# Folding weight pairs three steps behind their loads, and a fixed place for VectorE's loop head

## What is computed

```python
h = einsum(silu(gate) * value, w2)          # [3008 tokens, 1024], from g = silu(gate) * value
y = rms_norm(h, post_ln)                    # residual stream, written out
a = layer_norm(y) @ [wq_a | wkv_a].T        # 256 + 64 + 64 columns
q, ckv = rms_norm(a[:, :256]), rms_norm(a[:, 256:320])
k_pe = rope(a[:, 320:384])
```

## Time and profile before

| what | us |
|---|---|
| median of 3 runs (lowest, highest) | 2511.26 (2506.93, 2512.43) |
| the profiled execution, its own time | 2511.18 |
| its span (first to last instruction) | 2509.5 |
| of it: TensorE busy, VectorE busy | 2377.4, 1815.0 |
| this stage: first load of g to the first load of attention | 635.2 to 961.8 |

### The profile page before, as it was taken

One profiled execution on the slowest core, in us unless ns is written; L12 is line 12 of the kernel. 1 busy time (PEld: TensorE's weight loads), 2 busy tenths in 40 slices (PEclk: granted clock), 3 DMA queues, 4 the chain that ended last, 5 costly groups with the idle time before them and its releaser, 6 DMA issues. The chain is left out here.

```text
span 2509.5 us, 45975 instructions
## 1 busy us (share of the span) xinstructions
PE 2377.4 (95%) x14716; PEld 2061.9 (82%) x14716; DVE 1815.0 (72%) x3545; ACT 1246.3 (50%) x3736; POOL 1231.2 (49%) x1017
## 2 busy tenths in 40 slices
PE   8999999988699996999999999999999996999998
PEld 7888878776466676999999999878888885999998
DVE  8875586795446666898889898855776566777775
ACT  5664454442334545999999999922222222111110
POOL 5774675774013225677677767620676553111110
PEclk9999999999899998999999999989999998999999
DMA  7654576667556651111111111287788996211111
GB/s 251 209 175 127 183 258 226 214 227 265 165 170 198 198 188 59 48 43 56 50 55 45 51 56 54 70 284 225 213 252 244 284 288 224 71 68 68 67 67 51
DMA packets 318257, 379.44 MB, mean 151 GB/s; under 512 B 25472, under 2 KB 260480, under 8 KB 317952
## 3 DMA queue, kind: packets, MB, share of 16 engines
q1 hardware_dynamic: 310320, 349.67, 44.3%
q0 software_dynamic: 7184, 25.69, 2.6%
q10 hardware_dynamic: 576, 2.10, 0.3%
HBM read 295.59 MB, written 81.79 MB: 150 GB/s over the span
## 5 line engine op out<-in xcount | busy, mean ns | idle before, releaser
L1551 ACT ACTIVATE attn_prob<-attn_prob,attn_bias 94x94 f32<-94x94 f32 x1024 | 366.8, 361 | 47.3 <-DVE attn_bias L1627 46.0
L668 DVE TENSOR_TENSOR up_t_lo<-early_raw,up_t_hi 128x502 fp32r<-128x502 f32 (+1 forms) x210 | 222.1, 1060 | 142.8 <-ACT up_t_hi L575 140.6
L517 POOL TENSOR_TENSOR early_raw<-early_raw 128x502 f32<-128x502 f32 (+1 forms) x150 | 234.1, 1564 | 133.0 <-DVE up_t_lo L668 73.4
L1672 POOL TENSOR_TENSOR attn_prob<-attn_prob,attn_share 94x752 f32<-94x752 f32 x128 | 188.1, 1470 | 178.6 <-DVE attn_share L1635 178.6
L575 ACT ACTIVATE up_t_hi<-early_raw 128x502 fp32r<-128x502 f32 (+1 forms) x210 | 130.8, 623 | 281.1 <-POOL early_raw L517 158.5
L1911 POOL TENSOR_TENSOR early_raw<-early_raw 128x512 f32<-128x512 f32 x120 | 172.1, 1439 | 194.2 <-DMA early_raw<-o_t 194.0
L1946 DVE TENSOR_TENSOR out_t_lo<-early_raw,out_t_hi 128x512 fp32r<-128x512 f32 x168 | 158.5, 946 | 148.3 <-ACT out_t_hi L1925 147.5
L756 PE MATMUL up_ps<-up_t_lo,early_s_hi 128*128 128x502 f32 (+1 forms) x608 | 243.6, 401 | 18.3 <-DVE up_t_lo L668 16.1
L1925 ACT ACTIVATE out_t_hi<-early_raw 128x512 fp32r<-128x512 f32 x168 | 105.1, 631 | 302.2 <-POOL early_raw L1911 148.1
L757 PE MATMUL up_ps<-up_t_hi,early_s_lo 128*128 128x502 f32 (+1 forms) x608 | 240.5, 396 | 0.0
L758 PE MATMUL up_ps<-up_t_hi,early_s_hi 128*128 128x502 f32 (+1 forms) x608 | 239.8, 394 | 0.0
(11 more groups left out here) (261 smaller groups left out, 6697.0 us busy)
## 6 DMA issues: line engine op xcount, KB each, us to landing
early_raw<-o_t SPq DMA_DIRECT2D x288, 256.0 KB, 4.7
early_raw<-x_f SPq DMA_DIRECT2D x240, 251.0 KB, 3.6
shared_ring<-w SPq DMA_DIRECT2D x120, 256.0 KB, 3.9
early_raw<-x_f SPq DMA_DIRECT2D x120, 250.0 KB, 3.4
shared_ring<-wvo SPq DMA_DIRECT2D x96, 256.0 KB, 4.8
o_t<-attn_o_t SPq DMA_DIRECT2D x128, 188.0 KB, 1.9
shared_ring<-wo SPq DMA_DIRECT2D x32, 512.0 KB, 6.6
y<-early_raw POOLq DMA_DIRECT2D x24, 512.0 KB, 3.6
```

Source lines behind the costliest of these rows:

```text
L517: nc.gpsimd.tensor_tensor(both[n % 2][:, 0:w], a, b, SEVEN[i].op_b).then_inc(both_done, 1)
L668: nc.vector.tensor_tensor(t_lo[s % NT][:, 0:w], src, t_hi[s % NT][:, 0:w], ALU.subtract).then_inc(lo_done, 1)
L1551: last = nc.scalar.activation(prob[u % NPR][0:SEQ, h, part], prob[u % NPR][0:SEQ, h, part], ACT.Exp, bias=bias[u % 2][0:SEQ, n:n + 1], sca ...
L1672: nc.gpsimd.tensor_tensor(p4, p4, share[u % 2][0:SEQ, :].unsqueeze(2).broadcast_to((SEQ, 8, SEQ)), ALU.mult).then_inc(prob_done, 1)
```

## The change

Two values. Folds are done three steps behind their loads in place of two, which moves them to steps 3, 4, 6, 7, ... 21, 22, 24 and 25 on TensorE, ScalarE and GpSimd (SyncE's loads keep their steps). And VectorE's loop in this stage gets a fixed place for its first instruction.

```diff
@@ -877,7 +877,7 @@
         CENTRE_AT = 2
         DEPTH = 4
         U = 6
-        D_F = 2
+        D_F = 3
         FOLD = {0: 0, 1: 1, 3: 2, 4: 3}
         assert PAIRS == TILES // U * len(FOLD)
 
@@ -1198,7 +1198,7 @@
                 body(k, m)
                 link.fill()
 
-            run_steps(dve, TILES, DEPTH, U, step)
+            run_steps(dve, TILES, DEPTH, U, step, at=0)
```

## The result

The changed kernel takes 2613.02 us (median of 4 runs, 2612.14 to 2613.72) against 2510.66 before (4 runs): ratio 1.0408, 95% interval 1.0392 to 1.0425. The profiled execution took 2612.93 us, its span is 101.7 us longer than before. Forecast were 2606 us, 2560 to 2645, and slower with 0.93.

A forecast was written before the change was run, and what follows sets the result against it. TensorE, busy 95% of the span, was taken as the bound. Beginning -6, steps 4 and 5 +13.4, steps 6 to 23 +82.9 (loop head gain included) and end +5 made +95.3, so 2606 us, range 2560 to 2645.

The forecast's parts named there:

- The release a step too late: SyncE's pair load waits for TensorE's fold in the same step, delaying g behind it: three steps 44.7 us, 12.3 more.
- 3k+1: Second step of each group of three, with a fold and late g: 18.7 us before the clock term.
- 3k+2: Third step of each group of three, no fold but late g: 13.0 us.
- The clock: TensorE's lower clock after idle waits: 2.9 us per three steps, 1.8 of it for 3k+1, between 0 and 6.6.
- End: Steps 24 to 27: step 24 lags about 1 us, step 25 carries the last fold, 4 us; together +5.
- Beginning: Step 2 loses its fold and step 3 carries the first: 6 us of gain, between 0 and 8.
- Steps 4 and 5: First steps with late g: 33.5 us in place of 20.1, +13.4.
- Loop head: VectorE's standstills at its loop's back edge, steps 12 and 18, go: full gain of 8.3 us, nothing for the entry.
- A: Rival at the head of 3k+1 and 3k+2: g lands within 5.3 us of release, in time; 2502 us, chance 0.04.
- B: Rival on g's transfer: neighbours could be what costs; landing 6 us after release gives 2508 us; chance 0.03.
- C: Rival: only steps with a fold suffer, 3k+2 staying at 8.0 us; 2559 us, chance 0.08.
- D: Rival: the loop head edit fails and VectorE still stands still twice, 6 us each; 2618 us, chance 0.15.

The follow-up runs named there:

- e10: Changed kernel plus 20 and 14 extra matmuls, results unused, in TensorE's two idle times; 2589.79 us, ratio 1.033 to the kernel before.
- e3: Changed kernel (folds three steps behind, loop head placed) with SyncE issuing g one step earlier; 2498.46 us, ratio 0.9949 to the kernel before.
- e1: Changed kernel with folds back at two steps behind, so only the loop head's place remains; 2501.9 us, ratio 0.9965 to the kernel before.
- e2: Changed kernel without the loop head's fixed place, so only the later folds remain; 2611.21 us, ratio 1.0393 to the kernel before.
- e6: Changed kernel with the two loads of wo left out from the third pair on; 2516.16 us, ratio 1.0024 to the kernel before.
- e8: Changed kernel with folds two steps behind and VectorE's loop head on slot 210 in place of 0; 2506.52 us, ratio 0.9987 to the kernel before.
- e11: e3 without the loop head's fixed place; 2502.05 us, ratio 0.9975 to the kernel before.

## Why the prediction was right

- *The release a step too late.* Right in place, and in size nearly so. In 3k+1 g was to land 12.6 us into the step and fold_v to begin at 14.1; in the step shown they came at 12.9 and 14.1 (813.7 and 814.94, from 800.8), on average of the six at 12.2 and 13.4. TensorE's idle time before it was to be 6.4 and is 5.6 on average (6.5 in the step shown), at the end of 3k+2 4.6 and 4.6. ScalarE waits for g 14 times in steps 4 to 23, 10.2 us each, for 14 times 7 to 10. Without the low clock a group takes 44.55 us for 44.7 forecast (e10). Its terms are less exact: the six 3k+1 of e10 take 19.1, 16.7, 18.6, 16.7, 18.5 and 17.8 us (cut at SyncE's pair loads), 17.9 on average for 18.7 forecast, so that the other two steps have 26.65 for 26.0. The two errors nearly cancel.
- *The clock* was the term that was mis-sized: 2.9 us per group forecast, 3.6 measured. Step 3k+1 takes 20.1 us for 17.9 in e10, so 2.2 for 1.8 forecast, and the other two steps together 28.0 for 26.65, so 1.4 for 1.1. The idle time at the end of 3k+2 is paid for in step 3k: from 784.6 to 800.8 it runs at 0.72 though g is in time there, and it takes 16.2 us. 3k+2 itself (13.05 for 13.0) pays nothing, since it waits for g anyway. Six groups make 4 of the 7 us by which the forecast fell short.
- *End*: +5 forecast, +7.9 measured. I left the clock out of this part: steps 24 and on run at 0.72, before at 0.84. e3, with full steps before it, has +4.3 against before (+4.9 against e1). That the other 3.6 us are the clock's was not tried by itself.
- *Beginning*: -6 forecast, -5.2 measured; e3 shows that -11.7 was to be had where g is not late, beyond the bound of 8 that I gave.
- *Steps 4 and 5*: +11.3 for +13.4. Against this stand +1.5 us ahead of this stage, which the change does not touch and which the forecast put at 0.
- *Loop head*: the gain, 8.1 us for 8.3, is real where VectorE is needed at once (e1: 202.7 to 194.6). As a gain of the changed kernel it is not shown: the forecast of steps 6 to 23 (six groups without a standstill) holds, but e2, with the head as before, is not slower in all, and the 4.7 us more of its trace do not stand in the steps of the back edges. So the groups of 48 us stand with and without the head, and the sum would have been as good had the head done nothing. The two standstills of before are 5.54 and 6.3 us, not 5.5 both. The cost at the entry of the loop, which I put at nothing, is a standstill of 1.9 to 2.7 us (1.9 in the changed kernel, 2.7 in e1); e3 pays 1.4 of its 2.1.
- The sentence that these two are the only standstills at a back edge is too strong: in the last stage VectorE's L2144 has two of up to 2.0 us, shortly behind the back edges of its loop.
- *Rivals.* A (2502 us) is excluded as the case, but its threshold fits with e6, and e1 and e3 are about what it priced. B was wrongly dismissed in its mechanism: with two loads and three quarters of the bytes fewer ahead, g takes 4.5 us in the median in place of 8.2 (the 12 loads of g behind a pair in steps 6 to 23). It did not come true because the loads are there. C is excluded: 3k+2 takes 13.05 us and not 8.0. D priced two standstills at 6 us each on top; in e2, where they could have been, there are two, of 2.6 and 2.5 us, and the total shows nothing of them. The estimate of 2.6 us for g was worked out from a fit that the Trainium skill ("DMA: Bandwidth & Descriptors", "Anatomy of one DMA") gives for a DMA that GpSimd issues, and SyncE issues g. No run here had g alone; the traces have 7.5 to 9.6 us behind six loads and 4.2 to 5.4 behind four. On the head, the Trainium skill ("Runtime: NRT & Kernel Launch", "Instruction fetch mechanics") says that an engine holds two blocks of 256 instructions and fetches first when a branch leads outside them. The runs agree as far as they go: no standstill at the back edge with the loop in two blocks (0 and 70), and up to 6.2 us with three (e8).

## What to carry to other kernels

Before a consumer is moved a step later, follow its release through the in-order queue that it feeds: what costs may be a load that stands behind and has nothing to do with it. Here 2 to 3 in one constant cost about 100 us (e2). The same constant with the small load issued one step ahead gained 6 us (e11), and 12 with the loop head placed too (e3). A loop head is worth placing where the trace shows the engine standing still at the back edge with nothing to wait for (8 us in e1), and where g was late no gain of it is resolved.

## What the runs showed that I had not expected

- The cost of a late load does not grow in proportion: landings 6.4 to 7.0 us after the release cost about 2 us in three steps, landings at 12.2 and 11.5 cost 15.7. By the working of rival A the first 5.3 us fall beside TensorE's own work; this share was not measured by itself.
- One load's time depends on what stands ahead on its queue: 7.5 to 9.6 us from issue to landing behind six loads (steps 6 to 23 of the changed kernel), 4.2 to 5.4 behind four with a quarter of the bytes (e6).
- Two waits of TensorE, 5.6 and 4.6 us on average per 48, keep its granted clock at 0.85 over the whole 288.8 us, and matmuls whose results nobody uses gave 23 us back (e10, at 0.98).
